# Two score matmuls side by side as 64-row tiles of the array, with one max and one exp for both

## The chip, the cores and the metric

The kernel runs on one core of a Trainium2 chip. Its time is the device time of one execution in microseconds (us), and lower is better. Three runs took 1871.0 to 1872.67 us, median 1871.48.

## What is computed

Eight sequences of 512 tokens with 128 features pass three blocks: half a feed-forward block, a small dilated attention, and the same half block again. Inside the feed-forward block (`_L0_ffn_ref`) is what the change touches, an attention with 16 heads of 8 features, followed by 8 experts:

```python
x = jnp.transpose(xt + conv_b[None, :, None], (0, 2, 1))      # after a convolution over 3 tokens
qkv = x @ wqkv.T + bqkv
...
scores = jnp.einsum('bhqd,bhkd->bhqk', q, k) / jnp.sqrt(jnp.float32(dh))
attn = jax.nn.softmax(scores, axis=-1)
ctx = jnp.einsum('bhqk,bhkd->bhqd', attn, v)
...
x = layernorm(x + attn_out, ln1_g, ln1_b)
probs = jax.nn.softmax(x @ gate_w + gate_b, axis=-1)
h = jax.nn.relu(jnp.einsum('bsd,edf->bsef', x, w1) + b1)
y = jnp.einsum('bsef,efd->bsed', h, w2) + b2
moe_out = jnp.einsum('bse,bsed->bsd', probs, y)
x = layernorm(x + moe_out, ln2_g, ln2_b)
```

It runs twice for each of the 8 sequences, so there are 16 "units".

## The kernel before, in words

Every engine walks the same software pipeline. `run` makes 19 iterations (-1 to 17), `walk` divides each into 64 ticks, and in tick t a unit that was begun in this iteration does its step T = t, the one begun an iteration earlier its step T = 64 + t, and so on, older units first. In the middle of the program an iteration so holds three units at different stages. All order is written out by hand: each engine runs its instructions as listed, and semaphores are the only link between engines.

The steps of one unit that matter here:

- T = -24 to -16: the queries and keys, each split into three bf16 parts, go to DRAM (`parts_out`), and come back regrouped by SyncE's queue into the packed operands `Qp` and `Kp` (`LOADS_AT`, L363). For a head, 48 rows hold all the products of parts that are needed.
- T = 0 to 63, phase one: in each tick TensorE multiplies 128 queries of one head with its 512 keys into the bank `score1a` or `score1b` in turn (L1020), and VectorE takes the row maximum (L749). It contracts 96 rows, of which rows 48 to 95 are zero. After every 16 ticks (`NM_AT`) the negated maxima are transposed (L965), split into three bf16 parts by ScalarE and VectorE, and written by three small DMAs into rows 96 to 98 of `Qp` (L371).
- T = 24 to 87, phase two: TensorE makes the transposed scores, now with the maximum subtracted by these rows (L1013), into `score2a` or `score2b` in turn, and ScalarE takes the exponential (L601).
- T = 29 to 92, every fourth tick: four matmuls with the values, in four 32-column tiles of the array into `ctx_ps` (L1033). Below they are called the value group. Operands are fp32, and each such matmul shows as two records.
- T = 112 to 182: in each even tick three fp32r matmuls of 512 columns into `hid_ps` (L905, L906, L909) and three into `y_ps`; ScalarE makes `hid` from the former (L625), VectorE rounds it (L720), GpSimd makes the low part (L502).

The order on TensorE in an even tick is therefore: three `hid_ps`, three `y_ps` matmuls, then the scores; in an odd tick only scores, and in every second odd tick the value group. A score matmul may start when the bank that it writes has been read, and the wait says which read that is:

```python
wait(pe, s["a_exp"], u.count(64, k - 1))      # phase two: the exp before the last one
...
wait(pe, s["a_max"], u.count(64, T - 1))      # phase one: the max before the last one
```

Of the kernel before, what the change touches and what calls it, by code (L numbers as in the profile page):

```python
# [7 lines left out]
ALU = mybir.AluOpType  # L8
ACT = mybir.ActivationFunctionType
AX = mybir.AxisListType  # L10
# [19 lines left out]
PACK_LOADS = 16 * 2 * 3  # L30
SCORE_ROWS = 96
MAX_ROW = 96
# [32 lines left out]
def macaron(nc, x, Wq, bq, Wk, bk, Wv, bv, Wo, bo, conv_w, conv_b, wqkv, bqkv, wo, bo2, ln1_g, ln1_b,  # L65
            gate_w, gate_b, w1, b1, w2, b2, ln2_g, ln2_b, out):
    with ExitStack() as ctx:
# [10 lines left out]
        score1 = [psum("score1a"), psum("score1b")]  # L78
        score2 = [psum("score2a"), psum("score2b")]
# [34 lines left out]
        Qp, Kp = sb("Qp", [128, H, S], BF16), sb("Kp", [128, H, S], BF16)  # L114
        V = [sb(f"V{p}", [128, TC, H, DH + 1]) for p in range(2)]

        negmax = sb("negmax", [128, 2, HG * TC])
# [3 lines left out]
        rden = sb("rden", [128, TC, HG])  # L121
# [25 lines left out]
        turned_vec, turned_conv, turned_qkv, turned_wo = score1[0], score1[1], score2[0], score2[1]  # L147
# [17 lines left out]
        for n in """  # L165
            ld_x ld_vec ld_small ld_conv ld_qkv ld_wo ld_mid ld_bc
            zero_v k_zero pack_zero ident0 ident_ready held_dve held_sp consts pads_zero
# [4 lines left out]
            f_xn f_xT f_xh f_xl f_conv f_c f_ch f_cl f_qk f_p1 f_r1 f_p2 f_p3 f_v f_vs pack_in  # L172
# [24 lines left out]

        s["parts_out"] = [sem("q_parts_out"), sem("k_parts_out")]
# [76 lines left out]
        def hid_bank(u, n):  # L275

            return score1[0] if alone(u, n) and n % 2 else hid_ps
# [24 lines left out]
        LOADS_AT = ({-19: 0, -6: 1, 9: 2, 25: 3}, {-16: 0, -6: 1, 9: 2, 25: 3})  # L302
# [5 lines left out]
        def _(sp):  # L308
# [32 lines left out]
            def tick(T, u, t, i, i0):  # L341

                for k, at in ((0, 40 - TICKS), (1, 43 - TICKS)):
                    if T == at:
                        wait_sp(s["pack_in"], u.count(PACK_LOADS * G, 0))
# [4 lines left out]
                for k, (Tk, g) in [(k, at) for k in range(2) for at in LOADS_AT[k].items()]:  # L350
# [3 lines left out]

                    wait_sp(s["a_s2"], (u.n - 1) * 64 + 16 * g + 16)
                    wait_sp(s["pack_zero"], 2)
                    wait_sp(s["pack_in"], u.count(PACK_LOADS * G, PACK_LOADS * g + PACK_LOADS // 2 * k))
                    hs = slice(g * HG, (g + 1) * HG)
                    for row, n, part, step in RUNS_OF_PARTS[k]:
                        src = dram[k][part:part + (n if step else 1), :, hs, :].rearrange("a d h q -> a d (h q)")  # L360
                        if not step:
                            src = src.to_broadcast([n, DH, HG * S])
                        sp.dma_start((Qp, Kp)[k][row * DH:(row + n) * DH, hs, :].rearrange("p h q -> p (h q)"), src)\  # L363
                            .then_inc(s["pack_in"], 16)
# [751 lines left out]
```

## Time and profile before

| | us |
|---|---|
| median of 3 runs | 1871.48 |
| span of the profiled execution | 1872.3 |
| TensorE busy | 1730.1 (92%) |
| VectorE busy | 1392.8 (74%) |
| ScalarE busy | 1083.4 (58%) |
| GpSimd busy | 966.4 (52%) |
| mean granted clock of TensorE | 0.986 of full |

For the profiled execution no time is given besides its span, which lies 0.8 us over the median. A matmul's record is longer than what it occupies the array for (0.38 to 0.40 us, while the next one of a dense stream starts 0.22 or 0.23 us after it), so costs on TensorE are read from start to start.

### The profile page before, as it was taken

To read this page: it belongs to the slowest core of one execution; us is meant where nothing else is said; L and a number is where in the kernel's file an instruction comes from. 1 tells how busy PE (TensorE), PEld (TensorE's weight loads), DVE (VectorE), ACT (ScalarE), POOL (GpSimd) and SP (SyncE) were. 2 spreads that over 40 slices of the span, in tenths; PEclk is the share of its full clock that TensorE was granted. 3 is DMA by queue.
4 is the path that set the end of the run, shared out by engine and by line. 5 is a ranking of instruction groups with operands and counts; after the bars stand their busy time and mean duration, and the time that the engine had idled before them with its cause. 6 is when DMAs were issued, how large, how long until landed. Compare 5 with 4: busy or idle time off the path is not lost.

```text
span 1872.3 us, 34172 instructions
## 1 busy us (share of the span) xinstructions
PE 1730.1 (92%) x8605; PEld 962.6 (51%) x8752; DVE 1392.8 (74%) x2967; ACT 1083.4 (58%) x1964; POOL 966.4 (52%) x829
## 2 busy tenths in 40 slices
PE   3788999999999999998999899998999999999977
PEld 1224555545555555554555445554555555555555
DVE  4776777767777878776787767877778776767777
ACT  2466666656666656565565555655656566665633
POOL 5312556555655556564565645646456565655322
PEclk9999999999999999999999999999999999999989
DMA  4211112121211212121121211202112121210111
GB/s 124 77 50 56 48 31 75 33 65 35 71 45 35 74 42 73 42 75 45 37 74 38 81 43 38 79 28 82 47 32 81 32 75 36 70 40 29 35 35 29
DMA packets 89827, 100.01 MB, mean 53 GB/s; under 512 B 14928, under 2 KB 65920, under 8 KB 89600
## 3 DMA queue, kind: packets, MB, share of 16 engines
q1 hardware_dynamic: 88336, 93.40, 18.2%
q0 software_dynamic: 1280, 4.20, 0.8%
q8 instruction: 84, 1.38, 0.3%
q14 instruction: 127, 1.04, 0.2%
HBM read 77.63 MB, written 20.19 MB: 52 GB/s over the span
## 4 chain that ended last, share of the span: by engine, by line
PE 69%; DVE 19%; issue 7%; DMA 2%; ACT 2%; SPq 1%; DVEq 1%; POOL 0%; ACTq 0%; POOLq 0%
PE ctx_ps L1033 11%; DVE negmax L749 6%; PE score1a L1020 5%; PE score1b L1020 5%; PE hid_ps L905 5%; PE y_ps L905 5%; PE hid_ps L909 5%; PE y_ps L909 5%; PE y_ps L906 5%; PE hid_ps L906 4%; PE score2b L1013 4%; PE score2a L1013 4%; DVE x1n L709 3%; DVE hidh L720 2%; PE misc L905 1%
## 5 line engine op out<-in xcount | busy, mean ns | idle before, releaser
L502 POOL TENSOR_TENSOR hidl<-hid,hidh 128x512 fp32r<-128x512 f32 x456 | 590.2, 1294 | 626.2 <-DVE hidh L720 620.1
L625 ACT ACTIVATE hid<-hid_ps,cols 128x512 f32<-128x512 f32 x484 | 333.0, 688 | 400.4 <-PE hid_ps L909 384.0
L749 DVE TENSOR_REDUCE negmax<-score1a 128x1 f32<-128x512 f32 x512 | 350.3, 684 | 235.1 <-PE score1a L1020 232.4
L601 ACT ACTIVATE probs<-score2a 128x512 f32<-128x512 f32 x512 | 305.0, 596 | 151.6 <-PE score2a L1013 89.6
L749 DVE TENSOR_REDUCE negmax<-score1b 128x1 f32<-128x512 f32 x512 | 348.8, 681 | 31.3 <-PE score1b L1020 28.0
L601 ACT ACTIVATE probs<-score2b 128x512 f32<-128x512 f32 x512 | 303.4, 593 | 24.6 <-PE score2b L1013 24.0
L905 PE MATMUL hid_ps<-x1h,w1h 128*128 128x512 f32 x484 | 257.7, 533 | 15.6 <-issue 12.9
L1033 PE MATMUL ctx_ps<-probs,V 128*9 128x512 f32 x2048 | 270.8, 601 | 1.2
L720 DVE CAST hidh<-hid 128x512 fp32r<-128x512 f32 x512 | 245.1, 479 | 13.8 <-ACT hid L625 12.9
L1020 PE MATMUL score1a<-Kp,Qp 96*128 96x512 bf16 x512 | 200.1, 391 | 32.3 <-DVE negmax L749 14.6
L1020 PE MATMUL score1b<-Kp,Qp 96*128 96x512 bf16 x512 | 199.7, 390 | 21.5 <-DVE negmax L749 18.7
L905 PE MATMUL y_ps<-hidh,w2h 128*128 128x512 f32 x512 | 211.8, 414 | 7.7 <-DVE gated L731 7.3
L510 POOL TENSOR_TENSOR yacc<-yacc,gated 128x512 f32<-128x512 f32 x128 | 165.0, 1289 | 76.9 <-DVE gated L731 76.9
L909 PE MATMUL y_ps<-hidl,w2h 128*128 128x512 f32 x512 | 204.6, 400 | 0.0
L906 PE MATMUL y_ps<-hidh,w2l 128*128 128x512 f32 x512 | 203.5, 397 | 0.0
L906 PE MATMUL hid_ps<-x1h,w1l 128*128 128x512 f32 x484 | 193.3, 399 | 8.5 <-issue 8.5
L909 PE MATMUL hid_ps<-x1l,w1h 128*128 128x512 f32 x484 | 194.2, 401 | 1.7
L1013 PE MATMUL score2b<-Qp,Kp 128*128 128x512 bf16 x498 | 191.4, 384 | 0.8 <-ACT probs L601 0.4
L1013 PE MATMUL score2a<-Qp,Kp 128*128 128x512 bf16 x379 | 149.1, 393 | 3.5 <-DMA Qp<-m_parts 3.0
L905 PEld LDWEIGHTS hid_ps<-x1h,w1h 128*128 128x128 f32 x484 | 93.0, 192 | 96.2 <-issue 67.8
L1020 PEld LDWEIGHTS score1b<-Kp,Qp 96*128 96x128 bf16 x512 | 50.1, 98 | 148.2 <-DVE negmax L749 107.7
L905 PEld LDWEIGHTS y_ps<-hidh,w2h 128*128 128x128 f32 x512 | 97.3, 190 | 49.1 <-issue 18.3
(181 smaller groups left out, 2232.4 us busy)
## 6 DMA issues: line engine op xcount, KB each, us to landing
gate_b<-gate_dram SPq DMA_DIRECT2D x128, 256.0 KB, 3.7
q_parts_dram<-q_parts SPq DMA_DIRECT2D x48, 128.0 KB, 2.3
k_parts_dram<-k_parts SPq DMA_DIRECT2D x48, 128.0 KB, 2.3
Qp<-q_parts_dram SPq DMA_DIRECT2D x64, 96.0 KB
Kp<-k_parts_dram SPq DMA_DIRECT2D x64, 96.0 KB
gate_b<-in_L_ffn_w POOLq DMA_DIRECT2D x16, 256.0 KB, 4.0
Qp<-q_parts_dram SPq DMA_DIRECT2D x64, 64.0 KB
Kp<-k_parts_dram SPq DMA_DIRECT2D x64, 64.0 KB
```

Of the source, the lines that this page charges most:

```text
L502: pool.tensor_tensor(hidl[:, n % RING, :], hid[:, n % 2, :], hidh[:, n % RING, :].bitcast(F32), ALU.subtract).then_inc(s["h_lo"], 1)
L510: pool.tensor_tensor(ya[:], ya[:], gated[:], ALU.add).then_inc(s["y_acc"], 1)
L601: act.activation(probs[:, n % 2, j, :], score2[(T - P2_AT) % 2][:], ACT.Exp, scale=SCALE)\
L625: act.activation(hid[:, n % 2, :], hid_bank(u, n)[:], ACT.Relu, bias=col(n))\
L720: dve.tensor_copy(hidh[:, n % RING, :], hid[:, n % 2, :]).then_inc(s["h_hi"], 1)
L749: dve.tensor_reduce(negmax[:, g % 2, T % 16:T % 16 + 1], score1[T % 2][:], AX.X, ALU.max, negate=True).then_inc(s["a_max"], 1)
L905: pe.matmul(dst, hi, rhi, start=start, stop=False)
L906: pe.matmul(dst, lo, rhi, start=False, stop=False)
L909: return pe.matmul(dst, hi, rlo, start=False, stop=stop)
L1013: pe.matmul(score2[k % 2][:], Kp[:, g * HG + j, kc * 128:(kc + 1) * 128], Qp[:, g * HG + j, :], start=True, stop=True).then_inc(s["a_s2"], 1)
L1020: pe.matmul(score1[T % 2][:], Qp[0:SCORE_ROWS, h, qc * 128:(qc + 1) * 128], Kp[0:SCORE_ROWS, h, :], start=True, stop=True).then_inc(s["a_s ...
L1033: last = pe.matmul(ctx_ps[32 * j:32 * j + DH + 1, :], V[p][:, kc, g * HG + j, :], probs[:, n % 2, j, :], start=(kc == 0), stop=(kc == TC - 1))
```

## The change

Heads i and i + 8 form a pair. `Qp` and `Kp` hold the 48 rows of head i in partitions 0 to 47 and those of head i + 8 in partitions 64 to 111; the three maximum rows stand at 48 to 50 and 112 to 114. In each even tick TensorE makes the scores of both heads for one chunk, by two matmuls whose operands start at partitions 0 and 64, so that each uses 64 rows of the array and all its columns, into the two halves (two banks) of `score1` or `score2`. One reduction of 2 x 512 and one exponential of 2 x 512 read them. Nothing is done on scores in odd ticks; the value group stays there. `score1` and `score2` have two banks as before, but both are now written together and read together, so the next pair waits for the read of the pair just before it.

`Qp` and `Kp` exist twice, one for even and one for odd units. All loads of a unit are issued at T = -19 (queries) and T = -16 (keys), 12 DMAs each with the same bytes in all, instead of 3 and 3 at four places. The maxima are written by six DMAs of 8 rows of `m_parts` instead of three of 16. GpSimd no longer clears `Qp` and `Kp` at the start; VectorE sets ones in four quarters of `Kp`.

```diff
-PACK_LOADS = 16 * 2 * 3
-SCORE_ROWS = 96
-MAX_ROW = 96
+PAIRS = H // 2
+HALF = 64
+SCORE_ROWS = 48
+MAX_ROW = 48
+ALL_ROWS = MAX_ROW + 3
+LOAD_CHUNKS = ((0, 2), (2, PAIRS))
...
-        score1 = [psum("score1a"), psum("score1b")]
-        score2 = [psum("score2a"), psum("score2b")]
+        score1 = ctx.enter_context(nc.psum_tensor("score1", [128, 2, 512], F32))
+        score2 = ctx.enter_context(nc.psum_tensor("score2", [128, 2, 512], F32))
...
-        Qp, Kp = sb("Qp", [128, H, S], BF16), sb("Kp", [128, H, S], BF16)
+        Qp = [sb(f"Qp{p}", [128, PAIRS, S], BF16) for p in range(2)]
+        Kp = [sb(f"Kp{p}", [128, PAIRS, S], BF16) for p in range(2)]
...
-        LOADS_AT = ({-19: 0, -6: 1, 9: 2, 25: 3}, {-16: 0, -6: 1, 9: 2, 25: 3})
+        LOADS_AT = {(0, -19), (1, -16)}
...
-                    for part in range(3):
-                        sp.dma_start(Qp[MAX_ROW + part:MAX_ROW + part + 1, g * HG:(g + 1) * HG, :],
-                                     m_parts[:, part, :]).then_inc(s["a_m_in"], 16)
+                    for part in range(3):
+                        for half in range(2):
+                            at = HALF * half + MAX_ROW + part
+                            sp.dma_start(Qp[u.parity][at:at + 1, 2 * g:2 * g + 2, :],
+                                         m_parts[8 * half:8 * half + 8, part, :]).then_inc(s["a_m_in"], 16)
...
-                pool.memset(Kp[:].bitcast(F32), 0.0).then_inc(s["k_zero"], 1)
-                pool.memset(Qp[:].bitcast(F32), 0.0).then_inc(s["pack_zero"], 1)
...
-                    act.activation(probs[:, n % 2, j, :], score2[(T - P2_AT) % 2][:], ACT.Exp, scale=SCALE)\
+                    act.activation(probs[:, n % 2, 2 * j:2 * j + 2, :], score2[:], ACT.Exp, scale=SCALE)\
                         .then_inc(s["a_exp"], 1)
...
-                dve.wait_ge(s["k_zero"], 1)
-                dve.memset(Kp[MAX_ROW:MAX_ROW + 3].bitcast(F32), TWO_ONES).then_inc(s["pack_zero"], 1)
+                for p in range(2):
+                    for at in (HALF // 2, HALF + HALF // 2):
+                        dve.memset(Kp[p][at:at + HALF // 2].bitcast(F32), TWO_ONES).then_inc(s["pack_ones"], 1)
...
-                    dve.tensor_reduce(negmax[:, g % 2, T % 16:T % 16 + 1], score1[T % 2][:], AX.X, ALU.max,
+                    dve.tensor_reduce(negmax[:, g % 2, :, k % 8], score1[:], AX.X, ALU.max,
                                       negate=True).then_inc(s["a_max"], 1)
...
-                    wait(pe, s["a_exp"], u.count(64, k - 1))
-                    pe.matmul(score2[k % 2][:], Kp[:, g * HG + j, kc * 128:(kc + 1) * 128],
-                              Qp[:, g * HG + j, :], start=True, stop=True).then_inc(s["a_s2"], 1)
+                    wait(pe, s["a_exp"], u.count(32, k))
+                    for half in range(2):
+                        rows = slice(HALF * half, HALF * half + ALL_ROWS)
+                        last = pe.matmul(score2[:, half, :], Kp[p][rows, 2 * g + j, kc * 128:(kc + 1) * 128],
+                                         Qp[p][rows, 2 * g + j, :], start=True, stop=True)
+                    last.then_inc(s["a_s2"], 1)
...
-                    wait(pe, s["a_max"], u.count(64, T - 1))
-                    pe.matmul(score1[T % 2][:], Qp[0:SCORE_ROWS, h, qc * 128:(qc + 1) * 128],
-                              Kp[0:SCORE_ROWS, h, :], start=True, stop=True).then_inc(s["a_s1"], 1)
+                    wait(pe, s["a_max"], u.count(32, k))
+                    for half in range(2):
+                        rows = slice(HALF * half, HALF * half + SCORE_ROWS)
+                        last = pe.matmul(score1[:, half, :], Qp[p][rows, pair, qc * 128:(qc + 1) * 128],
+                                         Kp[p][rows, pair, :], start=True, stop=True)
+                    last.then_inc(s["a_s1"], 1)
```

TensorE's instructions in two neighbouring ticks of the loop, an even and an odd one with a value group, before (each row is one matmul, with the tensor that it writes, its two operands and its waits):

```order
L909 MATMUL y_ps<-hidl,w2h 128x512
...
L1013 MATMUL score2a<-Qp,Kp 128x512 [waits a_exp]
L62 REGISTER_ALU
L1020 MATMUL score1a<-Kp,Qp 128x512 [waits a_max]
L1013 MATMUL score2b<-Qp,Kp 128x512 [waits a_exp]
L62 REGISTER_ALU
L1020 MATMUL score1b<-Kp,Qp 128x512 [waits a_max]
L1033 MATMUL ctx_ps<-probs,V0 9x512 [waits a_ctx,a_exp]
L1033 MATMUL ctx_ps<-probs,V0 9x512 x3
L62 REGISTER_ALU
L905 MATMUL hid_ps<-x1h,w1h 128x512 [waits h_full]
```

And the same kind of place now:

```order
L922 MATMUL y_ps<-hidl,w2h 128x512
L67 REGISTER_ALU
L1029 MATMUL score2<-Qp0,Kp0 128x512 [waits a_exp,a_m_in]
L1029 MATMUL score2<-Qp0,Kp0 128x512
L67 REGISTER_ALU
L1041 MATMUL score1<-Kp0,Qp0 128x512 [waits a_max]
L1041 MATMUL score1<-Kp0,Qp0 128x512
L1056 MATMUL ctx_ps<-probs,V0 9x512 [waits a_exp]
L1056 MATMUL ctx_ps<-probs,V0 9x512 x3
```

The four scores, which took turns, stand as two pairs, and only the first of a pair waits. The number of matmuls is the same.

SyncE's queue around T = -19 of a unit (t = 45 to 51 of an iteration), before (DMAs with the shape that they write):

```order
L363 DMA Qp<-q_parts_dram 24x1x2048 [waits a_s2,pack_zero,pack_in]
L363 DMA Qp<-q_parts_dram 16x1x2048
L363 DMA Qp<-q_parts_dram 8x2048
L62 REGISTER_ALU [waits k_parts_out,a_s2,pack_zero]
L363 DMA Kp<-k_parts_dram 24x2048 [waits pack_in]
L363 DMA Kp<-k_parts_dram 16x2048
L363 DMA Kp<-k_parts_dram 8x2048
L62 REGISTER_ALU
L371 DMA Qp<-m_parts 1x16x128 [waits a_m3,pack_zero]
L371 DMA Qp<-m_parts 1x16x128 x2
```

And now (six rows for queries and nine for keys that go on in the same way are left out at the dots):

```order
L374 DMA Qp1<-q_parts_dram 24x1x1024 [waits a_s2,pack_ones]
L374 DMA Qp1<-q_parts_dram 16x1x1024
L374 DMA Qp1<-q_parts_dram 8x1024
...
L374 DMA Qp1<-q_parts_dram 24x1x3072
L374 DMA Qp1<-q_parts_dram 16x1x3072
L374 DMA Qp1<-q_parts_dram 8x3072
...
L374 DMA Kp1<-k_parts_dram 8x3072
L67 REGISTER_ALU
L383 DMA Qp0<-m_parts 1x8x128 [waits a_m3]
L383 DMA Qp0<-m_parts 1x8x128 x5
```

The maxima of the running unit's third group stand behind 24 loads for the next unit instead of 6, and are six DMAs themselves.

## Rows read from the trace of the kernel before

**Rows 1.** The page, busy time: us, share of the span, instructions

```profile
PE 1730.1 (92%) x8605; PEld 962.6 (51%) x8752; DVE 1392.8 (74%) x2967; ACT 1083.4 (58%) x1964; POOL 966.4 (52%) x829
```

**Rows 2.** The page, the chain that ended last, shares by engine

```profile
PE 69%; DVE 19%; issue 7%; DMA 2%; ACT 2%; SPq 1%; DVEq 1%; POOL 0%; ACTq 0%; POOLq 0%
```

**Rows 3.** Busy time by stretch: length, PE, PEld, DVE, ACT, POOL, clock, DMA

```profile
82.80:154.60 71.80, 61.84 (x318) 20.73 (x323) 51.10 (x106) 46.59 (x90) 14.03 (x15) 0.98 0.18 49
...
468.90:574.00 105.10, 102.67 (x528) 57.82 (x535) 77.98 (x171) 65.77 (x121) 61.21 (x51) 1.00 0.19 52
```

**Rows 4.** Timeline: start, duration, engine, instruction; scores with no value group

```profile
480.27 0.39 PE L1013 MATMUL score2a<-Qp,Kp 128*128 128x512 bf16 x1
480.28 0.10 PEld L1020 LDWEIGHTS score1a<-Kp,Qp 96*128 96x128 bf16 x1
...
480.49 0.38 PE L1020 MATMUL score1a<-Kp,Qp 96*128 96x512 bf16 x1
...
480.91 0.69 DVE L749 TENSOR_REDUCE negmax<-score1a 128x1 f32<-128x512 f32 x1 [0.38 <-PE score1a L1020]
```

**Rows 5.** Timeline of TensorE around a transpose of maxima and a value group

```profile
516.52 0.38 PE L1020 MATMUL score1a<-Kp,Qp 96*128 96x512 bf16 x1
516.78 0.28 PE L965 MATMUL misc<-ident,negmax 128*16 128x128 f32 x1
516.89 0.38 PE L1013 MATMUL score2b<-Qp,Kp 128*128 128x512 bf16 x1
517.20 1.05 PE L1033 MATMUL ctx_ps<-probs,V 128*9 128x512 f32 x8
518.18 0.39 PE L1020 MATMUL score1b<-Kp,Qp 96*128 96x512 bf16 x1
```

**Rows 6.** Timeline of TensorE from a value group's second half on

```profile
511.97 0.61 PE L1033 MATMUL ctx_ps<-probs,V 128*9 128x512 f32 x4
512.51 0.50 PE L905 MATMUL hid_ps<-x1h,w1h 128*128 128x512 f32 x1
512.85 0.40 PE L906 MATMUL hid_ps<-x1h,w1l 128*128 128x512 f32 x1
513.08 0.39 PE L909 MATMUL hid_ps<-x1l,w1h 128*128 128x512 f32 x1
```

**Rows 7.** The page's groups: count, busy, mean ns, idle before, releaser

```profile
L749 DVE TENSOR_REDUCE negmax<-score1a 128x1 f32<-128x512 f32 x512 | 350.3, 684 | 235.1 <-PE score1a L1020 232.4
L601 ACT ACTIVATE probs<-score2a 128x512 f32<-128x512 f32 x512 | 305.0, 596 | 151.6 <-PE score2a L1013 89.6
...
L1020 PE MATMUL score1b<-Kp,Qp 96*128 96x512 bf16 x512 | 199.7, 390 | 21.5 <-DVE negmax L749 18.7
```

**Rows 8.** Timeline: a reduction, and the matmul that waited for it

```profile
474.45 0.68 DVE L749 TENSOR_REDUCE negmax<-score1a 128x1 f32<-128x512 f32 x1
...
475.19 0.39 PE L1020 MATMUL score1a<-Kp,Qp 96*128 96x512 bf16 x1 [0.33 <-DVE negmax L749]
```

**Rows 9.** Timeline of the set-up: a reduction of 128 elements

```profile
33.69 0.27 DVE L688 TENSOR_REDUCE dil_mask<-heads 128x4 f32<-128x128 f32 x1
```

**Rows 10.** Timeline of SyncE's queue, one iteration: time spent issuing

```profile
484.29 1.97 SPq L363 DMA_DIRECT2D Qp<-q_parts_dram  x3
...
495.66 1.85 SPq L371 DMA_DIRECT2D Qp<-m_parts  x3
...
509.64 1.06 SPq L363 DMA_DIRECT2D Kp<-k_parts_dram  x3
```

**Rows 11.** The list of DMA issues: KB each, median us to landing

```profile
Qp<-m_parts SPq DMA_DIRECT2D x192, 4.0 KB, 1.7
```

**Rows 12.** Timeline: two long stretches of VectorE at the start, one later

```profile
6.70 7.60 DVE L709 TENSOR_SCALAR f_xn<-f_xn,f_mv,f_ve 128x128 f32<-128x128 f32 x4 [1.49 <-POOL f_ve L474]
...
20.71 3.47 DVE L678 MEMSET Kp<- 3x4096 f32 x1 [0.91 <-issue]
...
471.85 2.68 DVE L709 TENSOR_SCALAR x1n<-x1n,c_mv,c_ve 128x128 f32<-128x128 f32 x4
```

More of the change, by code:

```diff
@@ L196, in chunks @@
             return tile[:].rearrange("p (c d) -> p c d", c=TC)
+        s["pack_in"] = [sem(f"pack_in{k}") for k in range(len(LOAD_CHUNKS))]
         s["parts_out"] = [sem("q_parts_out"), sem("k_parts_out")]
@@ L275, in hid_bank @@
         def hid_bank(u, n):
-            return score1[0] if alone(u, n) and n % 2 else hid_ps
+            return score1[:, 0, :] if alone(u, n) and n % 2 else hid_ps[:]
         def wait_lo(eng, u, k):
@@ L353, in tick @@
                     wait_sp(s["parts_out"][k], u.count(48, 48))
[L355 to L364, printed above, removed]
+                    wait_sp(s["a_s2"], (u.n - 1) * 32)
+                    wait_sp(s["pack_ones"], 4)
+                    for chunk_in, (lo, hi) in zip(s["pack_in"], LOAD_CHUNKS):
+                        for half in range(2):
+                            for row, n, part, step in RUNS_OF_PARTS[k]:
+                                src = dram[k][part:part + (n if step else 1), :,
+                                              PAIRS * half + lo:PAIRS * half + hi, :]\
+                                    .rearrange("a d i q -> a d (i q)")
+                                if not step:
+                                    src = src.to_broadcast([n, DH, (hi - lo) * S])
+                                at = HALF * half + row * DH
+                                sp.dma_start((Qp, Kp)[k][u.parity][at:at + n * DH, lo:hi, :]
+                                             .rearrange("p i q -> p (i q)"), src).then_inc(chunk_in, 16)
                 if T - 2 in NM_AT:
@@ new lines, in tick @@
+                    wait(pe, s["a_exp"], u.count(32, k))
[4 more added lines that the diff above has]
+                    last.then_inc(s["a_s2"], 1)
+                if 0 <= T < 64 and T % 2 == 0:
+                    k = T // 2
+                    pair, qc = divmod(k, TC)
+                    for chunk_in, (first_pair, _) in zip(s["pack_in"], LOAD_CHUNKS):
+                        if qc == 0 and pair == first_pair:
+                            wait(pe, chunk_in, u.count(CHUNK_LOADS, CHUNK_LOADS))
+                    wait(pe, s["a_max"], u.count(32, k))
+                    for half in range(2):
+                        rows = slice(HALF * half, HALF * half + SCORE_ROWS)
+                        last = pe.matmul(score1[:, half, :], Qp[p][rows, pair, qc * 128:(qc + 1) * 128],
+                                         Kp[p][rows, pair, :], start=True, stop=True)
+                    last.then_inc(s["a_s1"], 1)
@@ L1025, in tick @@
                     g, kc = divmod(n, TC)
-                    wait(pe, s["a_exp"], u.count(64, 4 * n + 4))
+                    wait(pe, s["a_exp"], u.count(32, 2 * n + 2))
                     if n == 0:
@@ L1032, in tick @@
                     for j in range(HG):
-                        last = pe.matmul(ctx_ps[32 * j:32 * j + DH + 1, :], V[p][:, kc, g * HG + j, :],
-                                         probs[:, n % 2, j, :], start=(kc == 0), stop=(kc == TC - 1))
+                        half, pair = divmod(j, 2)
+                        last = pe.matmul(ctx_ps[32 * j:32 * j + DH + 1, :], V[p][:, kc, PAIRS * half + 2 * g + pair, :],
+                                         probs[:, n % 2, 2 * pair + half, :], start=(kc == 0), stop=(kc == TC - 1))
                     last.then_inc(s["a_pv"], 1)
```

68 lines of the change are left out of this document (35 added, 33 removed).

## The prediction, made before the changed kernel had run

> **What bounds the kernel now.** I read the busy times first. TensorE is busy 92% of the span and VectorE 74% [rows 1], and the chain that ended last runs through TensorE for 69% and through VectorE for 19% [rows 2]. These are averages, so I cut the span into iterations. From 468.90 to 574.00 TensorE is busy 102.67 of 105.10 us, VectorE 77.98 and ScalarE 65.77; from 82.80 to 154.60, where the experts do not run yet, TensorE is busy 61.84 of 71.80 and VectorE 51.10 [rows 3]. The reader should see two regimes. From tick 48 of iteration 1 to the end of iteration 15 TensorE sets the pace, 14.25 iterations in all. In iterations 0 and 1 nobody is full, and the round trips between engines set it.
>
> A busy TensorE row says little about what a matmul costs, so I went to the timeline. A score matmul starts at 480.27 and the next at 480.49 [rows 4]: 0.22 us each, four in two ticks, 0.88 us. Waits of TensorE on VectorE are small in sum: 18.7 us before all 512 matmuls into `score1b` [rows 7]. So in the main regime TensorE's own time is worth nearly its full price, and the other engines only have to keep up.
>
> **What the pairs save and what they add on TensorE.** If the two matmuls of a pair run at the same time in their halves of the array, a pair takes 0.22 us plus a small offset. No row has 64-row tiles. The nearest is the value group, whose matmuls lie in four 32-column tiles: from its start to the next instruction it takes 0.98 us (517.20 to 518.18) [rows 5], from the start of its second four records 0.54 (511.97 to 512.51) [rows 6], so the second four start 0.44 after the first. Eight records of 512 columns in 0.98 us, where one bf16 score alone takes 0.22: sharing between tiles is shown, for columns. I take 0.23 us per pair. The bounds are 0.22, and 0.44 if rows do not share.
>
> The change switches the array between tile shapes more often. From `score2b` to the value group it takes 0.31 us (516.89 to 517.20) instead of 0.22: 0.09 for going in. Coming out, the second four run 0.44 like the first and the next instruction starts after 0.54: 0.10. And if that is an fp32r matmul, its own weights show: 512.51 to 512.85 is 0.34, where the next step of the stream, to 513.08, is 0.23 [rows 6], so 0.11 more. A counter-example is the transpose of the maxima, 16 columns wide: in after 0.26 and out after 0.11, which is what a transpose takes anyway [rows 5], so 0.04 for both ways. I take the value group's prices, 0.09 in and 0.09 + 0.11 out (its 0.10 holds the offset of the four starts too), since it is a stream of full length like the scores; 0.04 for a round trip is the other bound.
>
> The sum for two ticks without a value group: before 0.88; after 0.09 + 2 x 0.23 + 0.20 = 0.75; saved 0.13. With a value group: before 0.88 + 0.09 = 0.97 up to the group; after 0.09 + 0.46 + 0.09 = 0.64; saved 0.33, and the way out is as before, except that in about six of 16 groups a bf16 score stood behind it, which hid the 0.11 (518.18), and now an fp32r matmul does: 0.6 us back per iteration. An iteration has 16 of each: 16 x 0.46 - 0.6 = 6.8 us, times 14.25 = 97 us. In iteration 16, where 12 pairs of phase two are left without phase one, the switches cost about what the pairs save: nothing.
>
> A rule that speaks against this: the Trainium skill, TensorEngine Tiling (Array Packing), Key Properties, says that a change of tiling mode drains the array. The rows agree as far as the value group goes (0.09 in, 0.10 out), and not for the narrow transpose. The same skill, TensorE: Matmul & The Clock Gate, What overlaps and what doesn't, says that a weight load overlaps a running matmul only for other rows of the array. The trace disagrees: the load for `score1a` starts at 480.28, 0.01 us after the start of `score2a`, on the same rows [rows 4]. That page's measured gain for four row tiles is 3.07 times; at that efficiency, an estimate, a pair would take 0.28 us and the saving would shrink to about 3.6 us per iteration.
>
> **VectorE and ScalarE.** A max of 512 takes 0.684 us [rows 7] and one of 128 0.27 [rows 9], so 1.08 ns per element, and one of 1024 takes 1.24. An exp of 512 takes 0.596 [rows 7]; one of 1024 at most 1.19, and with a fixed part of 0.13 as the max has it 1.06. Busy time falls by 32 x 0.13 = 4 us per iteration on each engine. Neither bounds, so I count nothing for it.
>
> **The new wait.** A pair waits for the read of the pair before it, where a score waited for the last but one. The loop from one pair to the next: 0.42 us from matmul to reduction (480.49 to 480.91) [rows 4], 1.24 for the max, 0.06 from the end of a reduction to the waiting matmul (475.13 to 475.19) [rows 8], 1.72 in all, and about 0.2 less for the exp. TensorE comes back to phase one after 0.20 + 6 x 0.23 + 0.09 + 0.23 + 0.23 = 2.1 us without and 3.1 with a value group. So it fits with 0.4 us to spare. Queued behind the waiting pair on TensorE are all matmuls of the experts. What can use up the spare time is other work of VectorE: per pair a cast of 0.42 to 0.48 that is ready only late, and a few blocks such as the 2.68 us normalisation [rows 12]. Over two pairs (5.25 us) VectorE owes 2 x (1.24 + 0.48) = 3.4, so a block up to 1.8 us is absorbed and the largest few overrun by up to 0.9. Such blocks stall TensorE today too (the 18.7 us). I take 0.8 us per iteration more, 11 us in all; between 0 and 4 per iteration.
>
> **SyncE's queue.** Three query loads are issued in 1.97 us, three key loads in 1.06, three maxima in 1.85 [rows 10], and a maxima DMA lands 1.7 us after issue [rows 11]. At T = -19 and -16 stand now 4 x 1.97 + 4 x 1.06 = 12.1 us of issue, then six maxima DMAs, 3.7, and landing: 17.5 us after t = 45. Phase two needs them at t = 56, 11 ticks later, and a tick is 105.1 / 64 = 1.64 us now, 1.54 after: 16.9. So about 0.7 us late once per iteration, 10 us in all. For the three other groups only 1.85 us is added, inside seven ticks of 1.54. Between 0 and 3 us per iteration.
>
> **The beginning.** GpSimd's two clears go, beside which four normalisations took 7.60 us instead of 2.68 [rows 12]: 4.9 saved. The ones in `Kp` take four memsets of 2048 words instead of one of 4096 in 3.47 us [rows 12], some 7 us: 3.5 lost. The first keys come behind 12 query loads instead of 3, 6 us of issue, of which part was a wait before: 3 lost. In iterations 0 and 1 the ticks take 71.80 / 64 = 1.1 us, the maxima DMAs come too late by 1.5 to 2 us in up to eight groups and by 5 at the bursts, but loads no longer stand in SyncE's queue at other times, and the round trip of 1.72 per pair is under the 2.2 of today. Together I take +6 us, between -8 and +25.
>
> **Sum.** 1872.3 - 97 + 11 + 10 + 6 = 1802 us, against the profiled 1872.3; the median lies 0.8 below it, within the rounding. A difference of 0.2% (3.7 us) is about what can be told from none here.
>
> **Rivals.**
> - *Switches are as cheap as the narrow transpose shows.* With 0.04 per round trip (0.02 each way) the savings are 0.38 and 0.45 per two ticks, 13.3 us per iteration, 190 in all; TensorE's interval falls to 1.9 us against the loop of 1.72, so waits on VectorE grow to about 3 us per iteration. 1872 - 190 + 43 + 16 = 1741. For it: rows 5. Against: the value group. Chance 0.1.
> - *The halves do not share the array, or are held up by writing two banks at once.* A pair takes 0.44: without a value group 0.09 + 0.88 + 0.20 = 1.17 for 0.88, with one 1.06 for 0.97; 16 x 0.38 + 0.6 = 6.7 us lost per iteration, 95 in all, and the other terms: 1994. It decides from 0.35 us per pair on. Against: the column tiles share. But those write different partitions of one bank, and these the same partitions of two. Chance 0.11.
> - *The single buffer takes it back.* If TensorE waits for the max or exp before every pair rather than at a few blocks, each 0.1 us of it costs 32 x 14.25 x 0.1 = 46 us; from 0.15 us per pair on the kernel is slower than before. At 0.2, 1802 + 91 = 1893. For it: spare time is only 0.4 us without a value group, and VectorE, at 78 - 4 of 98 us, has a cast and others in the same interval. Against: the cast ends before the next pair is there. Chance 0.13 for this side, and 0.05 for a wash near 1872.
> - *The forecast's own mechanism*, with its terms within bounds: 1760 to 1850. Chance 0.61.
>
> **Numbers.** The likeliest time is 1802. The range of 8 in 10 leaves out the case without sharing (0.11) and the last part of the cheap one (0.05) and reaches to the single buffer's case: 1735 to 1900. Faster by over 0.2%: 0.61 + 0.1, and 0.01 from the edges, 0.72. Within 0.2%: 0.05. Slower: 0.11 + 0.13 less the edges, 0.23.
>
> **What would show it.** In the timeline of the changed kernel: the two matmuls of a pair start within 0.05 us of each other (0.22 apart: not shared); from the last `y_ps` matmul to the first score about 0.32 us; 0.34 behind a pair in the fp32r stream; max 1.24 and exp 1.06 us; a main iteration of 98 to 100 us instead of 105.10; idle time of TensorE before pairs, put down to the max or the exp, of under 3 us per iteration; one wait on `m_parts` DMAs per iteration, under 1 us. I would be wrong if pairs start apart, if a switch costs over 0.2 us, or if TensorE waits at most pairs.

## The result: 2.0% slower, outside the forecast range

The changed kernel takes 1907.64 us (median of 4 runs, 1904.02 to 1913.55) beside 1871.24 us (4 runs) for the kernel before: 1.0196 times as long, 95% interval 1.0178 to 1.0214. The forecast was 1802, from 1735 to 1900, with 0.23 for slower. The profiled execution has a span of 1908.4 us.

The page of the changed kernel: busy time by engine, the chain that ended last by engine, and the four groups of the scores:

```profile
PE 1651.2 (87%) x8752; PEld 858.4 (45%) x8752; DVE 1343.1 (70%) x2458; ACT 1042.0 (55%) x1452; POOL 963.2 (50%) x827
...
PE 53%; SPq 13%; issue 12%; DVE 9%; DMA 6%; POOL 5%; ACT 2%; DVEq 0%; POOLq 0%; ACTq 0%
...
L761 DVE TENSOR_REDUCE negmax<-score 128x2 f32<-128x1024 f32 x512 | 626.1, 1223 | 356.2 <-PE score L1041 354.1
L612 ACT ACTIVATE probs<-score 128x1024 f32<-128x1024 f32 x512 | 524.5, 1024 | 255.0 <-PE score L1029 253.6
...
L1029 PE MATMUL score<-Qp,Kp 51*128 51x512 bf16 x1024 | 204.8, 397 | 86.9 <-DMA Qp<-m_parts 75.9
L1041 PE MATMUL score<-Kp,Qp 48*128 48x512 bf16 x1024 | 204.3, 396 | 65.2 <-DVE negmax L761 39.1
```

Against [rows 1, 2] every engine has less to do: TensorE 79 us less, VectorE 50, ScalarE 41. The span is longer all the same, so what grew is waiting, and the chain says whose: SyncE's queue and DMA, together 3% of it before, are 19% now, and TensorE fell from 69% to 53%. The wait is in the L1029 row: 75.9 us before scores of phase two, until the DMAs that write the maxima into `Qp` have landed. The forecast had 10 us for it.

Two iterations of the same kernel, from tick 36 of iteration 0 and from tick 36 of iteration 4, with the columns of [rows 3]:

```profile
98.20:186.30 88.10, 55.97 (x327) 16.27 (x329) 49.66 (x74) 43.79 (x58) 13.53 (x14) 0.85 0.15 40
505.50:611.80 106.30, 99.05 (x539) 51.09 (x535) 75.38 (x139) 63.25 (x89) 61.34 (x52) 0.97 0.19 51
```

To see where the time goes in the whole program I cut every kernel at the same instruction, the copy of the convolution's high part into `ch` (L575, L565 before), which stands at tick 36 of each iteration; the first is that of iteration -1. Iterations 6 to 13 also hold the merge block (`mid`); in the table they stand apart. All columns are in us and come from the starts of these copies in each trace; they stand here for all kernels so that the experiments can be read against them.

| kernel | median | start of 4th copy (iteration 2) | mean iteration, 2 to 5 | mean iteration, 5 to 13 (merge) |
|---|---|---|---|---|
| before | 1871.2 | 252.8 | 107.1 | 114.2 |
| changed | 1907.6 | 287.6 | 108.1 | 114.2 |
| `e1_spread` | 1871.8 | 258.7 | 103.5 | 115.6 |
| `e2_three_dmas` | 1895.4 | 282.2 | 107.7 | 113.1 |
| `e3_before_burst` | 2014.1 | 292.8 | 114.7 | 122.0 |
| `e4_spread_three` | 1836.1 | 251.2 | 101.9 | 113.2 |
| `e5_keys_after_mid` | 1797.8 | 248.9 | 101.7 | 108.1 |
| `e6_maxima_on_act` | 1900.3 | 283.5 | 108.1 | 113.6 |
| `e7_before_single_buffer` | 2264.0 | 326.2 | 131.4 | 136.5 |

The second row holds the result: 34.8 us are lost before the fourth copy, 3 more up to iteration 5, and nothing from there on. Two things have to be explained: a start that is 35 us longer, and main iterations that did not gain the 5 us each that the forecast gave them.

### The profile page after: what moved, and what is told of

Same layout as the page of the kernel before. It is cut to its first block, busy times and chain, and to the rows that moved or that the text cites. A ratio compares the mean times of both kernels' runs of the same rounds, so it can differ in the third digit from the quotient of the medians.

```text
span 1908.4 us, 30898 instructions
## 1 busy us (share of the span) xinstructions
PE 1651.2 (87%) x8752; PEld 858.4 (45%) x8752; DVE 1343.1 (70%) x2458; ACT 1042.0 (55%) x1452; POOL 963.2 (50%) x827
## 4 chain that ended last, share of the span: by engine, by line
PE 53%; SPq 13%; issue 12%; DVE 9%; DMA 6%; POOL 5%; ACT 2%; DVEq 0%; POOLq 0%; ACTq 0%
PE ctx_ps L1056 9%; SPq L374 9%; PE hid_ps L918 6%; DMA Qp<-m_parts 5%; PE score L1029 5%; PE y_ps L918 4%; PE y_ps L922 4%; PE y_ps L919 4%; PE score L1041 4%; PE hid_ps L922 4%; PE hid_ps L919 4%; SPq L383 3%; DVE negmax L761 3%; POOL hidl L512 2%; PE misc L969 2%
## 5 line engine op out<-in xcount | busy, mean ns | idle before, releaser
L761 DVE TENSOR_REDUCE negmax<-score 128x2 f32<-128x1024 f32 x512 | 626.1, 1223 | 356.2 <-PE score L1041 354.1
L612 ACT ACTIVATE probs<-score 128x1024 f32<-128x1024 f32 x512 | 524.5, 1024 | 255.0 <-PE score L1029 253.6
L1029 PE MATMUL score<-Qp,Kp 51*128 51x512 bf16 x1024 | 204.8, 397 | 86.9 <-DMA Qp<-m_parts 75.9
L1041 PE MATMUL score<-Kp,Qp 48*128 48x512 bf16 x1024 | 204.3, 396 | 65.2 <-DVE negmax L761 39.1
L732 DVE CAST hidh<-hid 128x512 fp32r<-128x512 f32 x512 | 244.6, 478 | 12.4 <-ACT hid L636 12.1
L918 PE MATMUL hid_ps<-x1h,w1h 128*128 128x512 f32 x484 | 236.8, 489 | 19.1 <-issue 15.6
L922 PE MATMUL hid_ps<-x1l,w1h 128*128 128x512 f32 x484 | 195.8, 405 | 12.8 <-DVE x1l L805 12.6
L1029 PEld LDWEIGHTS score<-Qp,Kp 51*128 51x128 bf16 x1024 | 49.1, 93 | 266.9 <-issue 144.4
L922 PEld LDWEIGHTS hid_ps<-x1l,w1h 128*128 128x128 f32 x484 | 93.4, 193 | 41.4 <-DVE x1l L805 19.7
L922 PEld LDWEIGHTS y_ps<-hidl,w2h 128*128 128x128 f32 x512 | 97.5, 190 | 23.7
L919 PEld LDWEIGHTS y_ps<-hidh,w2l 128*128 128x128 f32 x512 | 97.9, 191 | 21.3
L743 DVE SCALAR_TENSOR_TENSOR gated<-y_ps,cols,gate_b 128x512 f32<-128x512 f32 x128 | 95.4, 745 | 13.1 <-PE y_ps L922 11.4
```

What stands on the lines that cost most here:

```text
L612: act.activation(probs[:, n % 2, 2 * j:2 * j + 2, :], score2[:], ACT.Exp, scale=SCALE)\
L732: dve.tensor_copy(hidh[:, n % RING, :], hid[:, n % 2, :]).then_inc(s["h_hi"], 1)
L761: dve.tensor_reduce(negmax[:, g % 2, :, k % 8], score1[:], AX.X, ALU.max, negate=True).then_inc(s["a_max"], 1)
L918: pe.matmul(dst, hi, rhi, start=start, stop=False)
L919: pe.matmul(dst, lo, rhi, start=False, stop=False)
L922: return pe.matmul(dst, hi, rlo, start=False, stop=stop)
```

## The profile after: the pairs do what was forecast, the loads do not

TensorE's timeline in iteration 4 of the changed kernel (start, duration, engine, line, instruction; "x2" is a pair):

```profile
516.16 0.50 PE L918 MATMUL hid_ps<-x1h,w1h 128*128 128x512 f32 x1
516.49 0.40 PE L919 MATMUL hid_ps<-x1h,w1l 128*128 128x512 f32 x1
516.73 0.40 PE L922 MATMUL hid_ps<-x1l,w1h 128*128 128x512 f32 x1
...
535.76 0.40 PE L922 MATMUL y_ps<-hidl,w2h 128*128 128x512 f32 x1
536.09 0.39 PE L1029 MATMUL score<-Qp,Kp 51*128 51x512 bf16 x2
536.32 0.38 PE L1041 MATMUL score<-Kp,Qp 48*128 48x512 bf16 x2
536.63 0.66 PE L1017 MATMUL misc<-ident,yacc 128*128 128x128 f32 x4
...
542.11 0.61 PE L1029 MATMUL score<-Qp,Kp 51*128 51x512 bf16 x2 [3.43 <-DMA Qp<-m_parts]
542.51 0.64 PE L1041 MATMUL score<-Kp,Qp 48*128 48x512 bf16 x2
```

A pair takes 0.23 us from its start to the next one (536.09 to 536.32): two matmuls in the time of one, so the halves share the array. Behind the merged rows, the trace's single records of the two start 3 ns apart, where the forecast allowed 50. Going in costs 0.33 from the last `y_ps` matmul (535.76 to 536.09), where the forecast had 0.32; coming out 0.31 (536.32 to 536.63); and the first fp32r matmul behind a pair takes 0.33 (516.16 to 516.49) instead of 0.24. These prices on TensorE are within 0.01 us of the forecast.

The last two rows are tick 56, where phase two needs the maxima of heads in group 2. TensorE stood idle for 3.43 us. SyncE's queue in the same stretch (duration here is time spent issuing):

```profile
516.60 3.13 SPq L357 DMA_DIRECT2D k_parts_dram<-k_parts  x3
520.17 7.63 SPq L374 DMA_DIRECT2D Qp<-q_parts_dram  x12
528.07 4.29 SPq L374 DMA_DIRECT2D Kp<-k_parts_dram  x12
532.56 4.18 SPq L383 DMA_DIRECT2D Qp<-m_parts  x6
537.22 0.43 SPq L414 DMA_DIRECT2D resid<-in_L_attn_x  x1
```

The 24 loads are issued in 12.2 us (520.17 to 532.36), the forecast had 12.1. Their issue is not what makes the maxima late: VectorE makes the third part of the maxima at 531.9, in 0.27 us, and the first of the six DMAs goes out at 532.56. The last is issued at 536.74, and TensorE goes on at 542.11. That is 5.4 us behind the end of the last issue, and 6.0 behind its start at 536.1, from which [rows 11] counts its 1.7 to the landing (the moment when the DMA's semaphore tells that the data have arrived). What the DMA engines and TensorE do meanwhile, by stretch (length, PE, PEld, DVE, ACT, POOL, granted clock, mean busy share of the DMA engines, GB/s):

```profile
530.00:535.00 5.00, 4.68 (x29) 2.14 (x29) 4.22 (x9) 3.71 (x7) 2.31 (x2) 1.00 0.68 146
535.00:540.00 5.00, 3.68 (x19) 2.15 (x18) 3.20 (x12) 3.26 (x5) 2.95 (x4) 1.00 0.33 98
540.00:542.10 2.10, 0.00 (x0) 0.00 (x0) 0.00 (x0) 0.00 (x0) 1.02 (x1) 0.73 0.07 22
542.10:545.00 2.90, 2.89 (x13) 0.42 (x13) 1.56 (x2) 1.02 (x1) 0.17 (x1) 0.50 0.25 76
...
542.10:547.90 5.80, 5.79 (x23) 3.12 (x24) 2.35 (x4) 1.02 (x1) 2.50 (x2) 0.51 0.50 181
```

The 24 loads, issued in one piece, are called the burst below. The DMA engines are at 0.68 and then 0.33 while the maxima are on their way. What they carry can be told from the trace's records of single DMA packets (start, duration and size, not the engine; no row above shows them). Packets of 6144 bytes are rows of the loads of pairs 2 to 7, packets of 256 bytes rows of the maxima. From 530 to 535 the 6144-byte packets are 46.6 us of 54.0 us of work of the 16 engines. From 535 to 540 they are 9.5 of 26.7; about half is the load of `resid`, issued at 537.22 behind the maxima. After the last issue of the maxima 18 of them still run, 5.2 us together, so one or two at a time. The last two start at 539.73 and 540.12 and take 0.39 and 0.24 us, and the last maxima packets start at 540.37, when the latter is through. So the maxima did come behind the burst's data, the last of which only few engines still carried.

And the stall costs twice: TensorE's granted clock is 1.00 until 540.00, falls while the engine is idle, and is 0.50 (1.2 of 2.4 GHz) when it goes on, so a pair takes 0.40 us (542.11 to 542.51) instead of 0.23. From 542.10 to 547.90 TensorE works at a mean clock of 0.51, so 5.8 x 0.49 = 2.8 us go to it. With the stall of 3.43 and one of 0.67 for the next group that makes 6.9 us per iteration; without them 106.3 would be 99.4.

At the start, the first score and what follows on TensorE and VectorE:

```profile
57.17 0.61 PE L1041 MATMUL score<-Kp,Qp 48*128 48x512 bf16 x2 [25.46 <-DMA Kp<-k_parts_dram]
57.81 1.23 DVE L761 TENSOR_REDUCE negmax<-score 128x2 f32<-128x1024 f32 x1 [25.13 <-PE score L1041]
...
59.10 0.61 PE L1041 MATMUL score<-Kp,Qp 48*128 48x512 bf16 x2 [1.32 <-DVE negmax L761]
59.75 1.23 DVE L761 TENSOR_REDUCE negmax<-score 128x2 f32<-128x1024 f32 x1 [0.71 <-PE score L1041]
```

and the same place in the kernel before (rows that were not shown ahead):

```profile
44.36 0.58 PE L1020 MATMUL score1a<-Kp,Qp 96*128 96x512 bf16 x1 [10.78 <-DMA Kp<-k_parts_dram]
...
45.73 0.61 PE L1020 MATMUL score1a<-Kp,Qp 96*128 96x512 bf16 x1 [0.36 <-DVE negmax L749]
...
47.12 0.61 PE L1020 MATMUL score1a<-Kp,Qp 96*128 96x512 bf16 x1 [0.18 <-DVE negmax L749]
```

The first score comes 12.8 us later, since its keys stand behind all query loads: in SyncE's timeline those are issued from 32.32 to 40.23, all keys from 40.50 to 45.04. The issue explains the smaller part: even the last key load is out 12.1 us before the score starts, so here too it is the data that are late. Then, with one buffer, a pair takes 1.93 us (57.17 to 59.10) where two scores took 1.39 (45.73 to 47.12), with VectorE idle for 0.71 in each. Matmuls take 0.61 us in both kernels here, as they do at half clock at 542.11.

## The experiments

Theory A: the pairs gain what the forecast says, and the burst of 24 loads at T = -19 and -16 takes it back. In main iterations the maxima DMAs land late behind its data, at the start the first keys and the maxima do. Theory B: the pairs themselves, by their single buffer or their switches, are what costs. "Changed" below is the changed kernel of the diff.

### The loads in two steps (`e1_spread`)

Only the first two pairs' loads stay at T = -19 and -16; those of pairs 2 to 7 move behind the maxima DMAs.

```diff
-        LOADS_AT = {(0, -19), (1, -16)}
+        LOADS_AT = {(0, -19): 0, (1, -16): 0, (0, -7): 1, (1, -2): 1}
...
-                    for chunk_in, (lo, hi) in zip(s["pack_in"], LOAD_CHUNKS):
+                    for chunk_in, (lo, hi) in [(s["pack_in"][c], LOAD_CHUNKS[c]) for c in (LOADS_AT[k, Tk],)]:
```

> The changed kernel, with the 12 loads of pairs 2 to 7 moved from T = -19 and -16 to T = -7 and -2, so that they stand behind the maxima DMAs of T = 51 in SyncE's queue. Theory A (the burst of 24 loads in front of those DMAs stalls TensorE once per iteration, and delays the first keys): the wait of 3.4 us on m_parts at t = 56 goes, and with it the half clock behind it, some 6 us per main iteration (106 to 100), and the first score starts near 44 us instead of 57; in all 1800 to 1825 us. Theory B (the pairs themselves cost it: tile switches, the single buffer, the longer round trip): within 15 us of the changed kernel's 1908.

Measured 1871.77 us (10 runs, 1868.69 to 1876.33), 1.0012 times before (1.0002 to 1.0022), 36 us less than changed. The start of the fourth copy is at 258.7 instead of 287.6, iterations 2 to 5 take 103.5, and the first score starts at 41.65. The wait of scores on the maxima falls from 75.9 us to 16.3. But the merge iterations went up, to 115.6, with a wait that neither kernel had:

```profile
DVE m_st L708 <- DMA m_xn<-out: 48.2, 8, 8.4
```

So the stalls that theory A names are where it says. The total is in neither theory's range (A 1800 to 1825, B 1893 to 1923), as the edit brought a new wait of its own, 48.2 us of VectorE in 8 places.

### Three maxima DMAs instead of six (`e2_three_dmas`)

One DMA per part writes both halves. The loads stay as in changed.

```diff
-MAX_LOADS = 16 * 3 * 2
+MAX_LOADS = 16 * 3
...
-                        for half in range(2):
-                            at = HALF * half + MAX_ROW + part
-                            sp.dma_start(Qp[u.parity][at:at + 1, 2 * g:2 * g + 2, :],
-                                         m_parts[8 * half:8 * half + 8, part, :]).then_inc(s["a_m_in"], 16)
+                        at = MAX_ROW + part
+                        sp.dma_start(Qp[u.parity][at:at + HALF + 1:HALF, 2 * g:2 * g + 2, :]
+                                     .rearrange("t i (c q) -> t (i c) q", c=TC),
+                                     m_parts[:, part, :]).then_inc(s["a_m_in"], 16)
```

> The changed kernel, with three maxima DMAs of both halves at once instead of six, everything else as it is. Theory A with issue time as its limit: 1.9 us less on the queue before the last of them, so the wait at t = 56 falls from 3.4 to about 1.5 us, and iterations 0 and 1 gain too: 1870 to 1885 us. Theory A with the data of the loads as its limit (they sit in the same DMA engines until then): the wait stays near 3 us, 1895 to 1908 us. Theory B: no change beyond 5 us.

Measured 1895.41 us, 1.0139 times before (1.0113 to 1.0165): 12 us less than changed. The three DMAs are issued in 1.75 us instead of 4.18, yet the stall at tick 56 only falls from 3.43 to 3.01 us. That is what theory A expects with the data as its limit. Issuing faster takes hardly anything off the stall while the burst's data are under way.

### The burst alone, in the kernel before (`e3_before_burst`)

The kernel before with 18 more loads of the same shapes at T = -19 and -16, into a spare DRAM tensor that nothing reads. Unlike the change they are extra bytes, not moved ones.

```diff
+                    if g == 0:
+                        wait_sp(s[f"spare_in{k}"], u.count(16 * 9, 0))
+                        for part_of in range(3):
+                            for row, n, part, step in RUNS_OF_PARTS[k]:
...
+                                sp.dma_start(spare[k, row * DH:(row + n) * DH, HG * part_of:HG * (part_of + 1), :]
+                                             .rearrange("p h q -> p (h q)"), src).then_inc(s[f"spare_in{k}"], 16)
```

> The kernel before, unchanged in its matmuls and buffers, with 18 more loads at T = -19 and -16 (the bytes of the other 12 heads once more, into a spare tensor in DRAM that nobody reads), so that its maxima DMAs of T = 51 stand behind 24 loads as in the changed kernel. Theory A: a wait on m_parts at t = 56 of 1 to 3 us appears in every iteration (its own three DMAs are shorter), with half clock behind it, and the first score is late: 1871 grows by 30 to 90 us. Theory B: under 15 us more.

Measured 2014.13 us, 1.0762 times before (1.0734 to 1.0791). With no pair in the kernel, scores wait 101.5 us for the maxima (16 times) and 27.5 us for the first keys, beside 75.9 and 25.5 in changed; the fourth copy is 40 us late, an iteration takes 114.7. The signature of changed is made by the burst alone. The size is not as expected: 144 us more, where theory A had 30 to 90. It says less, since the bytes are extra and go to DRAM.

### Both edits (`e4_spread_three`)

The edits of `e1_spread` and `e2_three_dmas` together.

> Both edits at once, the loads spread and three maxima DMAs. Theory A: 5 to 20 us under the spread alone, from iterations 0 and 1, where ticks are short, and about nothing in the main iterations; 1790 to 1815 us. Theory B: as the changed kernel within 15 us.

Measured 1836.09 us, 0.982 times before (0.9801 to 0.9839), 36 us under the spread alone. Theory A had 5 to 20 and 1790 to 1815 in all, so the total is again in neither range: by the table, some 19 of the 36 us are gained in the merge iterations, where A expected nothing, and those are still slow. An iteration without merge block, and one with it:

```profile
457.20:557.10 99.90, 96.51 (x539) 49.85 (x535) 76.24 (x139) 63.10 (x89) 61.41 (x52) 1.00 0.19 54
669.90:785.20 115.30, 104.05 (x562) 54.28 (x558) 84.47 (x161) 65.19 (x91) 64.22 (x55) 0.96 0.20 54
```

The first is 5.2 us shorter than in [rows 3] at a full clock: the forecast's 98 to 100. The second has 11 us in which TensorE does nothing and a clock of 0.96. In it SyncE issues:

```profile
711.82 2.12 SPq L374 DMA_DIRECT2D Kp<-k_parts_dram  x6
714.12 0.43 SPq L417 DMA_DIRECT2D out<-resid  x1
715.06 0.41 SPq L427 DMA_DIRECT2D m_xn<-out  x1
```

VectorE waits for that last load, and TensorE for the max that is queued behind it on VectorE (the row of the waits, and of TensorE's timeline):

```profile
DVE m_st L708 <- DMA m_xn<-out: 6.8, 1, 6.8
```

```profile
727.38 0.61 PE L1041 MATMUL score<-Kp,Qp 48*128 48x512 bf16 x2 [6.26 <-DVE negmax L761]
```

It is the same pattern again at another place: a transfer that somebody needs at once stands behind loads that nobody needs for long. The page shows it on the store in front too, whose landing takes 7.8 us here and 3.8 in changed.

### The keys behind the merge block's load (`e5_keys_after_mid`)

The version of `e4_spread_three`, with one move more (the edit is shown against it).

```diff
-        LOADS_AT = {(0, -19): 0, (1, -16): 0, (0, -7): 1, (1, -2): 1}
+        LOADS_AT = {(0, -19): 0, (1, -16): 0, (0, -7): 1, (1, 6): 1}
```

> The spread loads and the three maxima DMAs of the version that took 1836 us, and the key loads of pairs 2 to 7 moved once more, from T = -2 (just in front of the store of the output and the load of m_xn for the merge block) to T = 6, behind both; the keys are needed at T = 16. Theory A (in iterations 6 to 13 VectorE waits 6.8 us for m_xn because those six loads' data lie in front of it, and TensorE waits 6.3 us for the max behind it): the wait of m_st on m_xn falls to under 2 us, these iterations from 112.9 to 106 to 108, the other iterations stay at 99.8, the total 1836 - 8 x 6 = about 1785 to 1800. Theory B (the single score bank in the chain with VectorE's merge work is what makes these iterations 113): they stay above 111 and the total within 10 us of 1836.

Measured 1797.83 us (1793.63 to 1800.11), 0.9605 times before (0.9589 to 0.9621). The same two iterations:

```profile
454.20:554.10 99.90, 96.50 (x539) 49.78 (x535) 76.25 (x139) 63.18 (x89) 61.49 (x52) 1.00 0.20 54
660.50:766.70 106.20, 101.20 (x562) 53.38 (x558) 84.50 (x161) 65.15 (x92) 64.51 (x55) 1.00 0.22 59
```

Merge iterations take 108.1 us in the mean instead of 113.2, the others are unchanged. VectorE's wait for `m_xn` fell from 27.7 us in all to 5.6, its longest from 6.8 to 2.4, a little over the 2 expected. Theory A holds: the total, the merge iterations and the others are as it said. This version beats both kernels: 110 us below changed by three edits that leave the pairs and their single buffer untouched.

### The maxima from ScalarE's queue (`e6_maxima_on_act`)

`e2_three_dmas`, with its three DMAs issued by ScalarE. It asks whether the maxima are late because of their place in SyncE's queue or because the engines that carry both are taken.

```diff
+                if T - 2 in NM_AT:
+                    g = NM_AT[T - 2]
+                    wait(act, s["a_m3"], u.count(4, g + 1))
+                    for part in range(3):
+                        at = MAX_ROW + part
+                        act.dma_start(Qp[u.parity][at:at + HALF + 1:HALF, 2 * g:2 * g + 2, :]
+                                      .rearrange("t i (c q) -> t (i c) q", c=TC),
+                                      m_parts[:, part, :]).then_inc(s["a_m_in"], 16)
```

SyncE no longer issues them.

> The changed kernel with three maxima DMAs that each write both halves, as in the version of 1895 us, but issued by ScalarE's queue instead of SyncE's; all 24 loads stay at T = -19 and -16. Theory A1 (the maxima DMAs are late because the DMA engines still carry the loads' data, whatever queue they come from): the wait of TensorE on the m_parts DMAs stays above 2 us at tick 56 of a main iteration, the iteration stays at 104 to 106 us, the total within 15 us of 1895. Theory A2 (they are late because they stand behind the loads in SyncE's own queue): the wait at tick 56 falls under 0.7 us, the main iteration to 100 or 101, and the total to 1840 to 1865. ScalarE pays 1.8 us of issue per group under both, at most 3 us per iteration.

Measured 1900.26 us, 1.0156 times before (1.0127 to 1.0184). ScalarE's queue, and the score that waits for it on TensorE:

```profile
528.35 1.66 ACTq L597 DMA_DIRECT2D Qp<-m_parts  x3
```

```profile
538.74 0.39 PE L1028 MATMUL score<-Qp,Kp 51*128 51x512 bf16 x2 [3.63 <-DMA Qp<-m_parts]
```

The last is issued at 530.01 and the score starts 8.7 us later; in `e2_three_dmas` these are 528.63 and 536.00, 7.4 us. SyncE's last load went out at 529.17, and its data go on: by the packet records the 48 maxima packets move only from 534.80 to 538.04, with load packets between them until one that starts at 537.49, takes 0.25 us and is followed by a maxima packet at 537.73. A queue of its own does not help: what is late is the work of the shared DMA engines, theory A1. Its numbers fit but for the iteration, which takes 106.3 us instead of 104 to 106. By the Trainium skill, DMA: Bandwidth & Descriptors, Queues, rings and completion order, the queues of SyncE and ScalarE use the same 16 engines, and a DMA's semaphore increment on an engine comes only after all earlier writes of that engine, whatever queue they are of. The trace agrees that the engines are shared, since the landing did not get shorter; whether the increments waited too it does not show, as the data themselves were late.

### The single buffer alone (`e7_before_single_buffer`)

```diff
-                    wait(pe, s["a_exp"], u.count(64, k - 1))
+                    wait(pe, s["a_exp"], u.count(64, k))
...
-                    wait(pe, s["a_max"], u.count(64, T - 1))
+                    wait(pe, s["a_max"], u.count(64, T))
```

> The kernel before, with its loads, its two banks per phase and its whole-array scores, but each score matmul waits for the max (or exp) of the score just before it instead of the last but one: the single buffer alone, without pairs. Theory A (the single buffer costs the main iterations little and the first two more): the loop of a score is 0.42 + 0.68 + 0.06 = 1.16 us against a tick of 1.64, so under 1.5 us more per main iteration; in iterations 0 and 1, where two scores took 1.40 us before, up to 0.9 us per two scores, 10 to 35 us in all; total 1885 to 1925. Theory B (the single buffer is what ate the pairs' gain everywhere): 3 us or more in each main iteration, total above 1930.

Measured 2263.98 us, 1.2077 times before (1.2035 to 1.212), far above theory A's 1885 to 1925. By its number alone this is theory B's outcome (above 1930, 3 us or more per main iteration). TensorE's scores of two neighbouring ticks show why:

```profile
704.53 0.38 PE L1013 MATMUL score2a<-Qp,Kp 128*128 128x512 bf16 x1
704.75 0.38 PE L1020 MATMUL score1a<-Kp,Qp 96*128 96x512 bf16 x1
705.88 0.39 PE L1013 MATMUL score2b<-Qp,Kp 128*128 128x512 bf16 x1 [0.74 <-ACT probs L601]
706.10 0.38 PE L1020 MATMUL score1b<-Kp,Qp 96*128 96x512 bf16 x1
```

My expectation spread the scores evenly, one per tick of 1.64 us. But the experts' six matmuls stand in even ticks only, so the scores of an even and an odd tick stand back to back at 0.22 us each [rows 4], and the odd tick's now wait for the read of the even one's: `score2b` starts 1.35 us after `score2a` (704.53 to 705.88) instead of 0.44. Not every place costs as much: TensorE waits for the exp before `score2b` 402 times, 222.5 us in all, and for the max before `score1b` 90 times, 69.5 us. The same iteration grows from 105.1 us [rows 3] to 128.2, and 73 us are lost before the fourth copy. The run so does not price the single buffer of the changed kernel, as I had meant it to, and it is no evidence for theory B there: `e5_keys_after_mid` has the changed kernel's single buffer and beats the kernel before. It shows something else: one buffer is cheap there only because a pair makes the scores of two ticks at once and leaves the odd tick empty, so two ticks share one round trip.

## Why the prediction was wrong, by its steps

- **What a pair takes, and the switches:** right. 0.23 us per pair, 0.33 in, 0.31 out, 0.33 for the first fp32r matmul behind it. The rival without sharing (1994) and the one with cheap switches (1741) both fall on the first rows of the timeline.
- **The saving per main iteration:** right once the loads are out of the way: 99.9 us for [rows 3]'s 105.10, in the forecast's 98 to 100, in `e4_spread_three` and `e5_keys_after_mid` alike. In the changed kernel itself it is 106.3.
- **Max and exp:** 1.223 and 1.024 us for 1.24 and 1.06.
- **The new wait on the single buffer:** small, as forecast. In `e5_keys_after_mid` TensorE waits 41.8 us for the max before 44 pairs of the whole program, some of it in the first iterations' round trips, and 11.3 us for the exp. In the kernel before these were 33.3 and 0.7, so it is 19 us more, where the forecast had 11.
- **SyncE's queue: this step failed.** Its sum of issue times was right (12.2 us for 12.1, 4.2 for 3.7). Its last term was not: "a maxima DMA lands 1.7 us after issue" was taken from a kernel in which hardly anything stands in front of it; here it was 6.0. From the start of the loads to the waiting score it took 21.9 us (520.17 to 542.11), not 17.5. And the price of being late was taken as the idle time alone. It was 4.1 us of idle time and about 2.8 of half clock per iteration, 6.9 together, where the forecast had 0.7 and at most 3. `e4_spread_three` against changed gives 6.2 (108.1 to 101.9).
- **The beginning: mis-sized.** +6, bounds -8 and +25; it was +31.7 by tick 36 of iteration 1 (186.3 for 154.6), and +34.8 by the fourth copy. I had 3 us for the first keys, and they are 12.8 late; scores wait 22.0 us for maxima up to 190, 13.3 of them in one place. The clears and memsets came out near the forecast: with them ScalarE starts on the query parts 1.9 us earlier (24.90 for 26.77), for 4.9 - 3.5 = 1.4. The loop was read wrongly: "under the 2.2 of today" does not hold at the start, where two scores took 1.39 and a pair takes 1.93. It costs something, but not the 32: `e4_spread_three` has it too, its first score starts 3.3 us before that of the kernel before (41.06 for 44.36), its third copy 2.1 behind (156.7 for 154.6), and its fourth at 251.2 is ahead again.
- **Together:** `e5_keys_after_mid` has a span of 1791.6, 116.8 us below changed: 38.7 of them before the fourth copy (287.6 to 248.9), 19 in the next three iterations, 49 in the eight merge iterations, 10 behind them. The distance between forecast and result is 106 us. So all of it is in the placement of the loads and in the six maxima DMAs instead of three: spreading alone gives 36 us, three DMAs alone 12, both 72, and the last move 38 more.
- **The rival of the right sign was the wrong one.** I gave 0.13 to a slower kernel by waits on the single buffer. None had the loads' data in front of the maxima as its mechanism, although the forecast's own sum from [rows 10] asked for it: 12 us of issue in one piece, just in front of DMAs that a score needs five ticks later.

Not settled: which of the DMA engines held the maxima up, and why the burst's last data lie on few of them. The packet records do not name the engine, and at 535.00 to 540.00 the mean is 0.33, so not all can have been full. Nor was it tried whether other placements are better still than T = 6 and -7.

## What to carry to other kernels

When a change gathers DMAs that were spread out, price not only their issue on the queue but where their data lie: whatever small transfer follows lands behind them, here from ScalarE's queue as from SyncE's. List for every DMA behind the burst who needs it and how many ticks later, and put loads that nobody needs yet behind those that somebody does; here two such moves, with three maxima DMAs for six, were worth 110 us, more than the 74 by which the best version beats the kernel before. And on TensorE add to a stall what the granted clock takes afterwards, which here was 2.8 us beside a stall of 3.43. A saving that shows in every busy time and not in the span is not lost: look for the wait that took it, and move that.

## What the runs showed of the hardware that was not expected

- Two matmuls of 48 or 51 rows in 64-row halves of the array, with 512 columns each into two banks, take 0.22 to 0.23 us together, as long as one matmul of 128 rows.
- Behind a burst whose last load had been issued 4.4 us before, the last of six DMAs of 2 KB landed 6.0 us after the start of its issue in the changed kernel, where one of 4 KB took 1.7 in the kernel before. Three of 4 KB were awaited for 7.4 us after their last issue (`e2_three_dmas`), and for 8.7 from a queue of their own (`e6_maxima_on_act`).
- After 3.43 us without work TensorE's granted clock stood at 0.50, and some 6 us of matmuls ran at that level: the first record at the usual length is that of 547.94. The fall need not come in the stall: in `e6_maxima_on_act`, after 3.63 us without work, the pair at 538.74 still took 0.23 us, and the value group behind it, at 539.28, took 1.59 instead of 0.98.
